# One-hots of the edge stage made on the scalar engine, transposes moved behind the sums

## The chip, the cores and the metric

The kernel runs on one core of a Trainium2 chip. The metric is the device time of one execution in microseconds; 3 runs of the kernel before gave 3189.21, 3190.27 and 3194.09 us. Engine names are those of the profile: PE is the matmul engine (PEld its weight loads), DVE the vector engine, ACT the scalar engine, POOL the GpSimd engine, SP the engine that issues loads.

## What is computed

A layer of a graph network over 6250 nodes of 256 features and 206250 edges. Cut to what matters:

```
edge_index = stack([src, dst]); xn = layernorm(x)
Wh = xn @ W.T + b                                   # 4 heads of 64
e = leaky_relu(alpha_src[i] + alpha_dst[j], 0.2)    # per edge (i, j) and head
att = exp(e - max_i e) / sum_i exp(e - max_i e)
x = x + segment_sum(att * Wh[j], i) + mix(xn)       # mix: linear attention, norms, gelu MLP
x = x + feed_forward(layernorm(x))                  # shared MLP and 2 of 4 experts
```

The mix part and the feed-forward part are dense; the segment sum gathers one row of Wh (and its scores) for each edge.

## The kernel before

A first stage (up to about 630 us of the trace) sorts the edges by blocks of 128 nodes and writes a table of Wh rows. The change is in the second stage, `stage_edges_and_feed_forward`, which works in **lots**: a lot is 8 tiles of 128 edges, all edges of a tile belonging to one node block. There are 234 lots, 6 in an iteration, so 39 iterations. For a lot n:

- POOL (`gathers`, L933) issues 8 indirect DMAs that bring 128 table rows each into one of 6 buffers; it may run 5 lots ahead of the sums.
- `select(n)` makes the lot's one-hot, 128 edges x 8 tiles x 128 nodes, in one of 3 buffers `onehot`: column equal to the edge's node number. Buffer n % 3 comes free when `sums(n - 3)` are done (`s_sum`).
- PE transposes it (`transposes`, L979, 8 matmuls into the bank `turned`), ACT copies it out (`turned_out`, L1182, into `onehot_t`), PE multiplies it by the block's scores (`by_node`, L989), which needs register loads of the block numbers first.
- DVE reduces and adds the scores (`weigh`, L1419 to L1425), ACT takes the exponential (`weights`, L1186), DVE multiplies the gathered rows by it (`product`, L1431, four of them).
- PE loads the bank numbers, clears a bank (`zero`, L995), and adds the lot up with 16 passes of one-hot times rows (`sums`, L1007). ACT copies a bank to `acc` (`block_out`, L1196) when the sums before are done.

Each engine runs its own list in program order. For lot n, `lot` writes into the lists: PE does `by_node(n+1)`, `transposes(n+2)`, a piece, `sums(n)`, a piece; ACT `block_out(n)`, `weights(n)`, `turned_out(n+2)`, two pieces; DVE `weigh(n)`, `select(n+2)`, a piece, `product(n)`, a piece. The pieces are dense work cut into 12 slots, two for each lot of an iteration. A loop over 11 batches (`all_segments`) has in each **round** one iteration with the pieces of a feed-forward batch (slots of `piece`), one with those of a mix batch (`mix`), and the plain iterations, without pieces, that the batch's edges still need: mostly one. Ahead of the loop stand two mix iterations, three plain ones and one feed-forward batch by itself. I call these iterations feed-forward, mix and plain, and number their lots 0 to 5: lot l has the slots 2l and 2l+1.

In the feed-forward iteration slot 4 transposes the normalised batch on PE, ACT copies it out (L1236, L1237), and a long row of matmuls follows. In the mix iteration slot 5 takes a square root on ACT for the first layer norm, which DVE finishes in slot 6 (L1555 to L1562) ahead of the products of lot 3; slot 8 transposes on PE, copies out on ACT and multiplies (L1022), slot 9 goes on with that.

Of the kernel before, what the change touches and what calls it, by code (L numbers as in the profile page):

```python
# [678 lines left out]
def stage_edges_and_feed_forward(nc, A, sh):  # L679
# [4 lines left out]
    with ctx:  # L684
# [16 lines left out]
        ident_bf = sb("ident_bf", [P, P], BF16)  # L701
        zeros = sb("zeros", [1, TB], BF16)
        t24 = sb("t24", [P, NBP, PIECE], BF16)
        t8_rest = dict(half=gathered[:, 0, 0:2, 0:NBP * H].rearrange("p k (b w) -> p b k w", w=H))
# [23 lines left out]
            "w_used", "w_col", "w_rows", "w_kept", "w_in", "w_sel", "w_tr", "w_ot", "w_as", "w_e", "w_exp", "w_sum"))  # L728
        s_dve = sem("s_dve2")

# [238 lines left out]
        def _(pe):  # L969
# [42 lines left out]
            def lot(it, l, piece):  # L1012
                by_node(*after(it, l, 1))
                transposes(*after(it, l, 2))
                piece(2 * l)
                sums(it, l)
                piece(2 * l + 1)

# [155 lines left out]
        def _(act):  # L1174
            s = nc.scalar

            def turned_out(it, l):

                n = number(it, l)
                act.wait_ge(s_tr, n + 1)  # L1180
                wait_freed(act, s_as, n - 1 if not isinstance(n, int) or n else 0)
                s.copy(onehot_t[:, l % 2, :, :].rearrange("p t e -> p (t e)"), turned[:, :]).then_inc(s_ot, 1)  # L1182
# [15 lines left out]
            def lot(it, l, piece):  # L1198
                block_out(it, l)
                weights(it, l)  # L1200
                turned_out(*after(it, l, 2))
                piece(2 * l)
                piece(2 * l + 1)
# [106 lines left out]
            load_mix(TAIL_BATCH)  # L1310
            turned_out(0, 0)
            turned_out(0, 1)
            act.wait_ge(s_w, 16 * LOADS3)
# [4 lines left out]
        def _(dve):  # L1318
# [85 lines left out]
            def select(it, l):  # L1404

                n = number(it, l)
                wait_freed(dve, s_sum, n - 2 if not isinstance(n, int) or n > 2 else 0)
                dve.wait_ge(s_col[l], 16 * it + 16)
                within = col[l][:, :, :, :].rearrange("p g k w -> p (g k) w")[:, :, 1:2].bitcast(F32)
                v.tensor_tensor(onehot[:, l % 3, :, :], iota_row[:, :].unsqueeze(1).broadcast_to([P, TILES, P]),  # L1410
                                within.broadcast_to([P, TILES, P]), ALU.is_equal).then_inc(s_sel[l], 1)

# [256 lines left out]
```

## Time and profile before

| | |
|---|---|
| median of 3 runs | 3190.27 us |
| the profiled execution | 3205.1 us, span 3203.4 us |
| PE busy | 2181.0 us (68%) |
| POOL busy | 2163.3 us (68%) |
| DVE busy | 1919.5 us (60%) |
| ACT busy | 753.7 us (24%) |
| mean granted clock of PE | 0.839 |

The edge stage takes the last 2570 us. Since every engine has a fixed order, busy shares alone do not tell what bounds it: one has to follow a lot from engine to engine in the timeline, and see which wait ends last.

### The profile page before, as it was taken

What the parts mean: (1) busy time and instruction counts of PE and PEld (TensorE: products, weight loads), DVE (VectorE), ACT (ScalarE), POOL (GpSimd) and SP (SyncE); (2) the same over time, 40 slices, a digit from 0 to 9 for tenths busy, and PEclk for the clock granted to TensorE, in tenths of its full rate; (3) what the DMA queues carried; (4) which work ended last, traced back from release to release, by engine and by line L of the source; (5) the groups of instructions that cost most, each with busy time, mean ns of one, the idle gap of its engine ahead of it and who ended that gap; (6) DMA issues with size and microseconds to landing.
All of it is one profiled execution on the core that took longest, in us unless ns stands there. A gap on an engine that the chain in (4) does not pass through costs nothing.

```text
span 3203.4 us, 40657 instructions
## 1 busy us (share of the span) xinstructions
PE 2181.0 (68%) x10817; PEld 1528.2 (48%) x10818; DVE 1919.5 (60%) x3954; ACT 753.7 (24%) x1346; POOL 2163.3 (68%) x2140
## 2 busy tenths in 40 slices
PE   0000687037778868787787978878768787787877
PEld 0000454025555555555555655555555555555554
DVE  8999554036565574656666465575654655756563
ACT  0000343012322222222222222222212222222222
POOL 0003777667777777777777777777777777777770
PEclk6555899568898998888889989898989888899988
DMA  5000122143434444444444434434444344344463
GB/s 183 0 0 1 54 72 66 18 118 91 116 92 105 121 102 123 100 110 113 103 122 101 121 103 104 124 101 123 102 105 123 98 111 117 99 124 102 122 93 31
DMA packets 271533, 305.63 MB, mean 95 GB/s; under 512 B 164258, under 2 KB 210856, under 8 KB 271080
## 3 DMA queue, kind: packets, MB, share of 16 engines
q0 software_dynamic: 97760, 251.60, 30.3%
q1 hardware_dynamic: 140098, 18.08, 3.8%
q10 hardware_dynamic: 33480, 33.36, 3.2%
q8 instruction: 122, 2.00, 0.3%
q14 instruction: 73, 0.60, 0.1%
HBM read 276.25 MB, written 26.62 MB: 95 GB/s over the span
## 4 chain that ended last, share of the span: by engine, by line
PE 34%; POOL 23%; issue 11%; DVE 9%; ACT 1%; DMA 1%; POOLq 0%; DVEq 0%; SPq 0%; ACTq 0%
POOL gathered L933 23%; PE sum_banks L1007 18%; PE f_banks L1022 7%; DVE onehot L1410 3%; PE turned L979 2%; PE f_banks L1066 1%; PE f_banks L1141 1%; DVE gathered L1431 1%; PE sum_banks L995 1%; DMA gathered<-table,col 1%; PE f_banks L1047 1%; PE f_banks L1142 1%; PE f_banks L1048 1%; DVE he L1559 1%; DVE he L1562 1%
## 5 line engine op out<-in xcount | busy, mean ns | idle before, releaser
L933 POOL DMA_INDIRECT gathered<-table,col x1872 | 1904.7, 1017 | 594.7 <-issue 564.5
L1007 PE MATMUL sum_banks<-gathered,onehot 128*128 128x260 f32 x3744 | 1060.8, 445 | 103.2 <-DVE gathered L1431 102.5
L1007 PEld LDWEIGHTS sum_banks<-gathered,onehot 128*128 128x128 f32 x3744 | 818.0, 224 | 292.2 <-issue 129.9
L1431 DVE TENSOR_TENSOR gathered<-gathered 128x512 f32<-128x512 f32 x936 | 591.5, 692 | 46.5 <-ACT gathered L1186 43.7
L1410 DVE TENSOR_TENSOR onehot<-iota_row,col 128x1024 f32<-128x1024 f32 x236 | 288.8, 1224 | 476.0 <-PE sum_banks L1007 447.9
L283 POOL DMA_INDIRECT edge_list<-payload,pos x244 | 247.1, 1013 | 349.9 <-DVE pos L400 273.0
L1182 ACT COPY onehot_t<-turned 128x1024 bf16<-128x1024 bf16 x236 | 238.7, 1011 | 398.0 <-PE turned L979 392.0
L1196 ACT COPY acc<-sum_banks x234 | 88.0, 376 | 870.3 <-PE sum_banks L1007 721.2
L979 PE MATMUL turned<-ident_bf,onehot 128*128 128x128 bf16 x1888 | 158.4, 231 | 188.9 <-DVE onehot L1410 188.8
L979 PEld LDWEIGHTS turned<-ident_bf,onehot 128*128 128x128 bf16 x1888 | 116.1, 103 | 207.0 <-DVE onehot L1410 168.9
L989 PE MATMUL scores<-t,onehot_t 128*128 x1880 | 102.2, 175 | 141.8 <-DVE scored L1419 98.8
L989 PEld LDWEIGHTS scores<-t,onehot_t 128*128 128x128 bf16 x1880 | 86.8, 97 | 219.3 <-issue 200.2
L644 PE MATMUL bank<-ident,y 128*128 128x128 f32 x56 | 8.2, 294 | 234.6 <-DVE y L482 234.6
L1419 DVE TENSOR_REDUCE scored<-scores 128x64 f32<-128x192 f32 x234 | 81.8, 350 | 101.3 <-DMA gathered<-table,col 86.0
L995 PE MATMUL sum_banks<-zeros 1*128 1x260 bf16 x236 | 70.6, 300 | 99.2 <-issue 92.2
L644 PEld LDWEIGHTS bank<-ident,y 128*128 128x128 f32 x56 | 7.0, 153 | 235.3 <-issue 235.3
L1022 PE MATMUL f_banks<-xT,wT_mix 128*128 128x512 f32 x208 | 94.9, 599 | 16.5 <-ACT xT L1294 16.5
L995 PEld LDWEIGHTS sum_banks<-zeros 1*128 1x128 bf16 x236 | 21.7, 92 | 166.2 <-issue 157.7
L1022 PE MATMUL f_banks<-xT,eW 128*128 128x512 f32 (+1 forms) x208 | 90.2, 568 | 0.0
L314 DVE TENSOR_SCALAR_CACHE_REDUCE xn_all<-xn_all,iota_row 128x1612 bf16<-128x1612 bf16 x49 | 88.9, 1891 | 1.8 <-POOL ones_row L273 1.8
L1219 ACT ACTIVATE he<-f_banks,eb 128x512 f32<-128x512 f32 (+1 forms) x78 | 51.3, 661 | 139.1 <-PE f_banks L1022 134.4
L354 DVE TENSOR_TENSOR xn_all<-xn_all 128x1024 f32<-128x1024 f32 x66 | 80.9, 1226 | 2.3
(316 smaller groups left out, 2499.8 us busy)
## 6 DMA issues: line engine op xcount, KB each, us to landing
gathered<-table,col POOLq DMA_INDIRECT x1872
xn_batch<-xn ACTq DMA_DIRECT2D x13, 512.0 KB, 4.4
x_all<-in_x SPq DMA_DIRECT2D x1, 6144.0 KB
x_batch<-in_x ACTq DMA_DIRECT2D x12, 512.0 KB
out<-xf ACTq DMA_DIRECT2D x12, 512.0 KB
edge_list<-xn_all SPq DMA_DIRECT2D x2, 2176.0 KB, 13.7
edge_list<-payload,pos POOLq DMA_INDIRECT x244
col<-edge_list SPq DMA_DIRECT2D x236, 8.0 KB, 2.1
```

Source lines behind the costliest of these rows:

```text
L283: g.indirect_dma_start(sh["windows"], bass.IndirectOffsetOnAxis(ap=pos[:, w:w + 1], axis=0), payload[:, w * Q:w * Q + Q, :].rearrange("p e ...
L314: v.tensor_scalar(hit[b % 2], bucket, iota_row[:, b:b + 1], 0.0, ALU.is_equal, ALU.add, accum_out=counts[:, b:b + 1]).then_inc(s_counts, 1)
L933: g.indirect_dma_start(gathered[:, l, t, :], None, sh["table"], bass.IndirectOffsetOnAxis(ap=col[l][:, t // G, t % G, 0:1], axis=0)).then_ ...
L979: last = t.transpose(turned[:, tile * P:tile * P + P], halves_of[:, l % 3, tile, :, 1], ident_bf[:, :])
L989: last = t.matmul(scores[:, tile * PIECE:tile * PIECE + PIECE], onehot_t[:, l % 2, tile, :], t24[:, ds(blocks[tile // G], 1), :].rearrange ...
L995: return t.matmul(sum_banks[:, bank, 0:TB].rearrange("p a w -> p (a w)"), zeros[:, 0:P], zeros[:, :], start=True, stop=False, skip_group_c ...
L1007: last = t.matmul(sum_banks[:, ds(banks_of[g], 1), 0:TB].rearrange("p a w -> p (a w)"), onehot[:, l % 3, g * G + k, :], gathered[:, l, g * ...
L1022: last = t.matmul(bank, left, right, start=i == 0, stop=i == len(pairs) - 1)
L1182: s.copy(onehot_t[:, l % 2, :, :].rearrange("p t e -> p (t e)"), turned[:, :]).then_inc(s_ot, 1)
L1196: s.copy(acc[:, ds(place, 1), :], sum_banks[:, ds(bank, 1), 0:TB]).then_inc(s_cp, 1)
L1410: v.tensor_tensor(onehot[:, l % 3, :, :], iota_row[:, :].unsqueeze(1).broadcast_to([P, TILES, P]), within.broadcast_to([P, TILES, P]), ALU ...
L1431: v.tensor_tensor(value, value, gathered[:, l, tiles, C:TB].unsqueeze(3).broadcast_to([P, G, H, HD]), ALU.mult).then_inc(s_mul, 1)
```

## The change

The one-hot is no longer made by DVE with one comparison. DVE only writes the negative node numbers of a lot (`minus`, 8 numbers a partition). ACT makes |column - node| tile by tile, 8 activations of 128 columns with a pointer bias into a bf16 buffer `apart`, waits for its own writes, and then takes relu(1 - that) over all 1024 columns into `onehot`. PE transposes lot n+2 behind the sums of lot n, not ahead of them, and ACT's copy of the transposed one-hot stands behind the even piece instead of ahead of it.

```diff
@@ tiles and semaphores
+        apart = sb("apart", [P, TILES, P], BF16)
+        minus = sb("minus", [P, LOTS, TILES, 1])
-        s_dve = sem("s_dve2")
+        s_dve, s_minus, s_apart = sem("s_dve2"), sem("s_minus"), sem("s_apart")
@@ PE
             def lot(it, l, piece):
                 by_node(*after(it, l, 1))
-                transposes(*after(it, l, 2))
                 piece(2 * l)
                 sums(it, l)
+                transposes(*after(it, l, 2))
                 piece(2 * l + 1)
@@ ACT
+            def select(it, l):
+                n = number(it, l)
+                act.wait_ge(s_minus, n + 1)
+                wait_freed(act, s_sum, n - 2 if not isinstance(n, int) or n > 2 else 0)
+                wait_freed(act, s_sel[(l + LOTS - 1) % LOTS], it + 1 if l else it)
+                for tile in range(TILES):
+                    last = s.activation(apart[:, tile, :], iota_row[:, :], ACT.Abs, bias=minus[:, l, tile, :])
+                last.then_inc(s_apart, 1)
+                act.wait_ge(s_apart, n + 1)
+                s.activation(onehot[:, l % 3, :, :], apart[:, :, :], ACT.Relu, bias=1.0, scale=-1.0)\
+                    .then_inc(s_sel[l], 1)
@@ ACT
             def lot(it, l, piece):
                 block_out(it, l)
                 weights(it, l)
+                select(*after(it, l, 2))
+                piece(2 * l)
                 turned_out(*after(it, l, 2))
-                piece(2 * l)
                 piece(2 * l + 1)
@@ ACT, ahead of all lots
-            turned_out(0, 0)
-            turned_out(0, 1)
+            for l in range(2):
+                select(0, l)
+                turned_out(0, l)
@@ DVE
             def select(it, l):
-                wait_freed(dve, s_sum, n - 2 if not isinstance(n, int) or n > 2 else 0)
+                wait_freed(dve, s_sel[l], it)
                 dve.wait_ge(s_col[l], 16 * it + 16)
                 within = col[l][:, :, :, :].rearrange("p g k w -> p (g k) w")[:, :, 1:2].bitcast(F32)
-                v.tensor_tensor(onehot[:, l % 3, :, :], iota_row[:, :].unsqueeze(1).broadcast_to([P, TILES, P]),
-                                within.broadcast_to([P, TILES, P]), ALU.is_equal).then_inc(s_sel[l], 1)
+                v.tensor_scalar(minus[:, l, :, :], within, -1.0, None, ALU.mult).then_inc(s_minus, 1)
```

On PE, before, from the scores of one lot to the sums of the next piece of the list (lot 5 of the mix iteration):

```order
L989 ISA
L989 MATMUL scores<-t,onehot_t 128x24 x2
L979 MATMUL turned<-ident_bf,onehot 128x128 x8
L800 TENSOR_LOAD lots
L995 ISA
L995 MATMUL sum_banks<-zeros 128x260
L1007 ISA
L1007 MATMUL sum_banks<-gathered,onehot 128x260 x2
```

and on PE after, from the scores of the same lot to its first sums:

```order
L991 ISA
L991 MATMUL scores<-t,onehot_t 128x24 x2
L802 TENSOR_LOAD lots
L997 ISA
L997 MATMUL sum_banks<-zeros 128x260
L1009 ISA
L1009 MATMUL sum_banks<-gathered,onehot 128x260 x2
```

The eight transposes have left this place and stand behind the sums, so that the next item of the list, the scores of the following lot, comes straight after them.

On ACT, before, lots 4 and the start of 5 of the mix iteration (L1294 the copies of slot 8, L1298 its gelu):

```order
L1196 COPY acc<-sum_banks 128x260
L1186 ACTIVATE gathered<-e 128x8x4
L1182 COPY onehot_t<-turned 128x1024
L1294 COPY xT<-f_banks 128x512 x2
L1298 ACT_TABLE_LOAD
L1298 ACTIVATE he<-f_banks,b_col 128x512 x2
```

and after:

```order
L1210 COPY acc<-sum_banks 128x260
L1200 ACTIVATE gathered<-e 128x8x4
L1185 ACTIVATE apart<-iota_row,minus 128x128 x8
L1188 ACTIVATE onehot<-apart 128x1024
L1309 COPY xT<-f_banks 128x512 x2
L1313 ACT_TABLE_LOAD
L1313 ACTIVATE he<-f_banks,b_col 128x512 x2
L1196 COPY onehot_t<-turned 128x1024
L802 TENSOR_LOAD lots x2
```

The nine activations of the one-hot stand ahead of the copies that slot 8 waits for, and the copy of the transposed one-hot behind them, right ahead of the next lot's bank copy. The list of ACT holds 39 table loads before and 39 after, at the same neighbours.

## Rows read from the trace of the kernel before

**Rows 1.** Waits: who waited for whom, total us, times, longest us.

```profile
PE turned L979 <- DVE onehot L1410: 188.8, 176, 28.5
...
DVE scored L1419 <- DMA gathered<-table,col: 86.0, 30, 7.8
...
POOL gathered L933 <- PE sum_banks L1007: 30.2, 21, 5.6
...
PE scores L989 <- ACT onehot_t L1182: 3.4, 2, 1.8
```

**Rows 2.** Groups: line, engine, op xcount | busy us, mean ns | idle before, releaser.

```profile
L933 POOL DMA_INDIRECT gathered<-table,col x1872 | 1904.7, 1017 | 594.7 <-issue 564.5 <-PE sum_banks L1007 30.2
```

**Rows 3.** Chain in order of time: start us, us, what.

```profile
1783.63 5.33 PE f_banks L1022 x8
...
1974.77 5.56 PE f_banks L1022 x8
...
2413.61 6.29 PE f_banks L1022 x8
```

**Rows 4.** Timeline of two plain lots: start us, us, engine, line, operation [idle before].

```profile
1539.39 3.77 PE L1007 MATMUL sum_banks<-gathered,onehot 128*128 128x260 f32 x16
...
1543.19 1.23 DVE L1410 TENSOR_TENSOR onehot<-iota_row,col 128x1024 f32<-128x1024 f32 x1 [1.55 <-PE sum_banks L1007]
...
1543.58 0.23 ACT L1186 ACTIVATE gathered<-e 128x32 f32<-128x32 f32 x1
...
1544.48 0.62 PE L979 MATMUL turned<-ident_bf,onehot 128*128 128x128 bf16 x8 [1.13 <-DVE onehot L1410]
1545.13 1.01 ACT L1182 COPY onehot_t<-turned 128x1024 bf16<-128x1024 bf16 x1 [1.32 <-PE turned L979]
...
1545.99 0.28 PE L995 MATMUL sum_banks<-zeros 1*128 1x260 bf16 x1 [0.90 <-issue]
...
1546.21 3.77 PE L1007 MATMUL sum_banks<-gathered,onehot 128*128 128x260 f32 x16
...
1549.82 0.35 PE L989 MATMUL scores<-t,onehot_t 128*128 x8
```

**Rows 5.** Timeline of POOL in the next plain lot.

```profile
1549.35 0.94 POOL L933 DMA_INDIRECT gathered<-table,col  x1 [0.30 <-issue]
1550.60 1.56 POOL L933 DMA_INDIRECT gathered<-table,col  x1 [0.30 <-issue]
```

**Rows 6.** Timeline of the mix iteration, lots 2 and 3.

```profile
1481.10 0.35 PE L989 MATMUL scores<-t,onehot_t 128*128 x8
...
1481.81 1.28 ACT L1186 ACT_TABLE_LOAD   x1
1482.44 0.17 DVE L1555 RECIPROCAL inv<-std 128x4 f32<-128x4 f32 x1
...
1485.40 2.50 DVE L1431 TENSOR_TENSOR gathered<-gathered 128x512 f32<-128x512 f32 x4
...
1486.23 2.14 PE L1007 MATMUL sum_banks<-gathered,onehot 128*128 128x260 f32 x6 [1.84 <-DVE gathered L1431]
```

**Rows 7.** Timeline of the mix iteration, lot 4.

```profile
1491.52 0.35 PE L989 MATMUL scores<-t,onehot_t 128*128 x8
...
1495.95 3.70 PE L1022 MATMUL f_banks<-xT,wT_mix 128*128 128x512 f32 x8 [1.27 <-ACT xT L1294]
```

**Rows 8.** Timeline of the feed-forward iteration, lots 1 and 2.

```profile
1389.59 0.38 ACT L1196 COPY acc<-sum_banks  x1 [4.42 <-PE sum_banks L1007]
...
1394.77 0.59 ACT L1236 COPY xT<-f_banks 128x512 f32<-128x512 f32 x1 [0.69 <-PE f_banks L1059]
```

**Rows 9.** Groups by shape, one on ACT.

```profile
L1219 ACT ACTIVATE he<-f_banks,eb 128x128 f32<-128x128 f32 x6 | 2.0, 367 | 0.3
```

**Rows 10.** Windows, two stretches: us, busy us by engine, granted clock (PEclk).

```profile
1533.00:1556.00 23.00, 18.03 (x116) 14.57 (x117) 15.30 (x33) 4.65 (x10) 17.74 (x18) 1.00 0.42 105
2343.00:2373.00 30.00, 20.67 (x99) 15.34 (x99) 13.67 (x27) 4.48 (x8) 22.99 (x24) 0.83 0.41 104
```

## The prediction

> **What bounds the kernel now.** I read the waits first. POOL, the engine that issues the gathers, waited for PE only 21 times, 30.2 us in all, and DVE waited for a gather before 30 of 234 lots only, 86.0 us [rows 1]. So in most lots the rows are there and the lot waits for the engines. POOL itself needs (1904.7 + 594.7) / 234 = 10.68 us a lot [rows 2], 192 us for the 18 lots of a round of the loop (feed-forward, mix and plain iteration). The chain has the same heavy matmul piece at 1783.63 and 1974.77 [rows 3]: 191.1 us a round. The two are level. What makes POOL quicker brings nothing unless the chain gets quicker too; what lengthens the chain costs in full as soon as the gathers' lead is used.
>
> The chain of a plain lot is in rows 4. Sums start at 1539.39, the next at 1546.21. Behind the sums DVE makes a one-hot (1543.19, 1.23 us), PE waits 1.13 us for it, transposes (0.62), waits 0.90 for its register load, clears the bank and sums. A step is 6.82 us; the register wait is 0.25 us in every other lot, so the mean is 6.5 us. ACT's copy of the transposed one-hot (1545.13, 1.01 us) runs under the sums; the scores waited for it twice in the whole run, 3.4 us [rows 1]. The wait for the one-hot is 188.8 us in all [rows 1]: that is what the change can win.
>
> **The change, part by part.** The diff frees PE from the wait for the one-hot of lot n+2, but puts three things in series that ran under the sums: transposes, ACT's copy, and, through ACT's fixed order, the bank copy and the exponential of the next lot.
>
> *Plain lots.* From the start of the sums: 3.61 us until PE's next item (1546.21 to 1549.82), 0.65 from the start of the transposes to the copy (1544.48 to 1545.13), copy 1.01 [rows 4]: 5.27 us. From there two branches. ACT and DVE: bank copy 0.38 [rows 8], exponential 0.23 [rows 4], first product and its signal 0.83 (1485.40 to 1486.23) [rows 6]: 6.7 us. PE: the scores may start only now, and their register load, till now hidden, is exposed; I price it like the one behind it, 0.25 to 0.90. So 0.25 to 0.90, scores 0.35, 0.25 to 0.90, and 0.22 from clearing to sums [rows 4]: 6.3 to 7.6 us. With the hand-overs between engines I take 7.4, because two loads in series rarely both take the short time: 0.9 us more than 6.5. Bounds 6.7 (the other branch) and 8.0 (long loads, hand-overs of 0.1 to 0.2). Lot 0 behind a branch of the loop waits for instructions anyway and gets nothing: five lots, +4.5 us (1 to 7.5) for a plain iteration.
>
> *The one-hot on ACT.* One activation of 128 columns with a pointer bias took 0.367 us [rows 9], eight 2.9 us, less where they overlap; say 2.2 to 2.9. The relu over 1024 columns is like the copy of 1024, 1.01 us [rows 4]. With the wait between, 3.4 us (3.3 to 4.0). In a plain lot it lies under the sums: ACT is free from 5.9 us to the next copy at 4.3 + 7.4 = 11.7 us, where 3.4 fit. The number of table loads does not change. On DVE 1.23 us goes and a write of 8 numbers comes; DVE bounds nothing there. By the Trainium skill, ScalarE: Activation LUTs, section What ACT_TABLE_LOAD costs, an activation with a pointer bias takes about 280 ns plus 0.833 ns a column and neighbours overlap by 93 ns. As an estimate the one-hot would then be 3.5 us, and the sum the same within 1 us a round; the row of 0.367 us agrees with its 0.387.
>
> *Mix iteration.* Lot 3: from the end of lot 2's sums (1481.10) to lot 3's (1486.23) are 5.13 us [rows 6]. Today ACT has taken the root before that. After, the root stands behind the copy that waits for the transposes: 0.65 + 1.01, table load 1.28, root about 0.2 (like the exponential), then DVE from the reciprocal to the product 2.96 (1482.44 to 1485.40) and 0.83 [rows 4, 6]: 6.95, so +1.8 (1.4 to 2.2). Lot 4: end of sums 1491.52 to the slot's matmuls at 1495.95, 4.43 us [rows 7]. After: 0.65 + 1.01 + 0.38 + 0.23, the one-hot 3.4, two copies of 0.59 that overlap a little (1.1): 6.8, so +2.35 (2 to 3). The transposes behind lot 4's sums add 0.5, since there the matmuls of slot 9 follow at once. Lots 0 to 2 gain about 1.5 us of waits for the one-hot and lose half of it to transposes behind the sums: -0.8. Together +3.8 (2 to 6).
>
> *Feed-forward iteration.* Lot 2: ACT's bank copy at 1389.59 to its copy for slot 4 at 1394.77, 5.2 us [rows 8]. After: 0.65 + 1.01 before the bank copy, then 0.38 + 1.28 + 0.23 + 3.4: 6.95, so +1.7. In lots 3 to 5 two sets of transposes leave a place where PE waited for ACT and stand behind sums with work queued: +0.7. Lots 0 and 1 lose the one-hot's 1.23 us ahead of the products and gain ACT's later start: 0. Together +2.3 (1 to 4).
>
> *Sum.* A round gets 4.5 + 3.8 + 2.3 = 10.6 us longer; 11 rounds +117. Ahead of the loop stand two mix and three plain iterations: 2 x 3.8 + 3 x 4.5 = 21, of which 4 fall where lots wait for gathers today: +17. One round has one more plain iteration: 2413.61 - 1974.77 = 438.8 us for two rounds [rows 3] leaves 56.6 for it, 9.4 a lot, the pace of the gathers. A late chain finds its rows waiting and takes 6 x 7.4 = 44: -12. The last lot waits 7.8 us for its gathers today [rows 1], not then: -7. In all +115. The span of 3203.4 becomes 3318; the profiled execution stands 14.8 us over the median, so the forecast is 3190 + 115 = **3305 us**. With the low bounds a round costs 4 and the total is +25 (3215); with the high ones 17.5 and +208 (3398).
>
> **Rivals.** *Faster.* POOL's gathers are stretched where DVE works from two SBUF tiles: 0.94 us each, but 1.56 for one beside a one-hot (1550.60) [rows 5]. All stretches together are 1904.7 - 1872 x 0.94 = 145 us [rows 2], and I give the one-hots two thirds, 90 us. If the chain shortens by its 188.8 us of waits and gains none, POOL is the bound and the time 3190 - 90 = 3100. It decides at a plain lot of 6.5 us: the mechanism wins only if scores and register loads behind ACT's copy take less than the 1.13 us that PE waits now. Against it: the copy alone is 1.01 and nothing covers it. Chance 0.11. The Trainium skill, SBUF — State Buffer, section Who interferes with whom, holds that two SBUF inputs on DVE contend with GpSimd's reads but infers that descriptor generation goes on. By that, this rival's gain from POOL would be nil and its time about 3190; the trace's 1.56 us speaks against it.
>
> *No change* (0.04): low bounds everywhere, and a faster pace of the gathers in the first rounds: 3190.
>
> *A colder PE* (0.15). In plain lots that follow each other closely the granted clock is 1.00 with PE busy 18.03 of 23 us; in plain lots that wait for gathers it is 0.83, busy 20.67 of 30 [rows 10]. PE's share in my 7.4 us lot is (3.61 + 0.62 + 0.35 + 0.28) / 7.4 = 66%, nearer to the second. There a lot costs PE 20.67 / 3 = 6.9 us instead of 18.03 x 6.5 / 23 = 5.1: 1.8 more in about 70 plain lots, 3305 + 126 = 3430.
>
> **How the numbers follow.** The forecast's case, the chain longer at full clock, has 0.70. The range of 3215 to 3440 takes in its bounds and the colder case; it leaves out faster, no change (together 0.15) and 0.05 above. A measurement tells 0.2%, 6 us, from no change. Faster 0.11, same 0.04, slower 0.85.
>
> **What would show it.** Right: scores waiting for ACT's copy more than 200 us in all, against 3.4; POOL waiting for the sums in every round; the wait of transposes for the one-hot near zero; plain steps of about 7.4 us; a round of about 202 us; gathers mostly 0.94 us without being worth anything. Wrong: if plain steps stay at 6.5 (faster), if the one-hot takes over 5 us and the transposes wait for it (slower than the range), or if ACT's register loads and not its activations fill its period.

## The result and the profile after

The changed kernel takes **3595.52 us** (median of 4 runs, 3590.64 to 3601.07), the kernel before 3191.26 beside it (3189.21 to 3194.09): a ratio of 1.1267, 95% interval 1.1247 to 1.1287. The direction was forecast, the size was not: +404 us instead of +115, and outside the range.

The profiled execution has a span of 3596.0 us. Below: busy time by engine, then the groups, of the changed kernel (operation, xcount | busy us, mean ns | idle before, releaser). In the changed file the gathers are L935, transposes L981, scores L991, zeroing L997, sums L1009, one-hots L1185 and L1188, ACT's copy of the turned one-hots L1196, the exponential L1200, the bank copy L1210.

```profile
PE 2368.9 (66%) x10817; PEld 1664.8 (46%) x10818; DVE 1667.7 (46%) x3954; ACT 1551.5 (43%) x3470; POOL 2093.5 (58%) x2140
```

```profile
L935 POOL DMA_INDIRECT gathered<-table,col x1872 | 1835.0, 980 | 1039.7 <-issue 535.5 <-PE sum_banks L1009 504.1
...
L1009 PE MATMUL sum_banks<-gathered,onehot 128*128 128x260 f32 x3744 | 1172.1, 481 | 154.0 <-DVE gathered L1446 152.2
...
L1185 ACT ACTIVATE apart<-iota_row,minus 128x128 bf16<-128x128 f32 x1888 | 574.3, 389 | 36.1 <-DVE minus L1426 36.0
```

And the same group of the sums before the change:

```profile
L1007 PE MATMUL sum_banks<-gathered,onehot 128*128 128x260 f32 x3744 | 1060.8, 445 | 103.2 <-DVE gathered L1431 102.5
```

The gathers became a little shorter (980 ns against 1017, [rows 2]) and worth nothing, for POOL now waits for the sums: 504.1 us against 30.2 [rows 1]. The same 3744 matmuls of the sums cost 111 us more; their number and shape are unchanged, and the windows below show the clock. The waits after (who for whom: total us, times, longest):

```profile
PE scores L991 <- ACT onehot_t L1196: 220.3, 128, 2.1
...
PE sum_banks L997 <- issue: 121.5, 114, 1.4
...
DVE recip L1478 <- ACT acc L1210: 87.8, 11, 8.4
...
PE turned L981 <- ACT onehot L1188: 33.3, 2, 31.0
```

and the row of the zeroing before the change:

```profile
PE sum_banks L995 <- issue: 92.2, 137, 1.0
```

The wait of the transposes for one-hots is down from 188.8 us to 33.3 (nearly all of it once, at the start), the wait of the scores for ACT's copy is up from 3.4 to 220.3 [rows 1], and DVE has a new wait for ACT, 8 us in each round. PE's wait for its own queue ("issue") ahead of the zeroing is not new; it rose by 29 us in all, so where it matters has to be read lot by lot. The chain of the kernel after, which answers to [rows 3]:

```profile
1748.74 6.10 PE f_banks L1024 x8
...
2417.74 6.11 PE f_banks L1024 x8
...
2700.42 6.42 PE f_banks L1024 x8
```

From the first to the second row are three rounds, (2417.74 - 1748.74) / 3 = 223.0 us each, against 191.1. Two plain lots of the kernel after, PE and one ACT row, which answer to [rows 4] (start us, us, engine, line, operation, [idle before]):

```profile
1670.54 0.28 PE L997 MATMUL sum_banks<-zeros 1*128 1x260 bf16 x1 [1.34 <-issue]
1670.76 5.46 PE L1009 MATMUL sum_banks<-gathered,onehot 128*128 128x260 f32 x16
...
1676.05 0.61 PE L981 MATMUL turned<-ident_bf,onehot 128*128 128x128 bf16 x8
1676.70 1.01 ACT L1196 COPY onehot_t<-turned 128x1024 bf16<-128x1024 bf16 x1 [4.80 <-PE turned L981]
...
1678.34 0.58 PE L991 MATMUL scores<-t,onehot_t 128*128 x8 [1.68 <-ACT onehot_t L1196]
...
1679.59 0.28 PE L997 MATMUL sum_banks<-zeros 1*128 1x260 bf16 x1 [0.67 <-issue]
1679.90 3.77 PE L1009 MATMUL sum_banks<-gathered,onehot 128*128 128x260 f32 x16
```

The order is the predicted one: sums, transposes, copy, scores, zeroing, in series. Two sizes are not. The zeroing waits 1.34 or 0.67 us behind the scores for nothing but PE's own queue ("issue"), and the first of these two sums takes 5.46 us instead of 3.77. Windows inside it (us; busy PE, PEld, DVE, ACT, POOL; granted clock, DMA share, GB/s):

```profile
1670.70:1671.70 1.00, 1.00 (x5) 0.86 (x5) 0.93 (x4) 0.97 (x2) 0.69 (x2) 1.00 0.41 133
...
1672.70:1673.70 1.00, 1.00 (x4) 0.81 (x3) 0.00 (x0) 0.00 (x0) 0.88 (x1) 0.50 0.44 83
...
1675.70:1676.70 1.00, 0.96 (x11) 0.63 (x9) 0.00 (x0) 0.00 (x1) 0.69 (x2) 1.00 0.44 133
```

The clock is at its upper level, 2.4 GHz, when the sums begin, falls to 1.2 GHz about a microsecond later, and is back before the sums end. In the 3.80 us ahead of these sums PE was busy for 0.77 us only, and the granted clock there was still 1.00.

What PE waits for under "issue" is a register load. These are PE's and ACT's loads in the kernel before (duration min/median/max in ns):

```profile
L800 ACTq TENSOR_LOAD <-lots x468: 271/278/1437, 689.3 to 3140.5; - x156
...
L800 PEldq TENSOR_LOAD <-blk x235: 327/332/348, 687.2 to 3149.9; - x118
L800 PEldq TENSOR_LOAD <-lots x234: 585/1030/1255, 691.6 to 3151.8; - x117
```

PE's load of the bank numbers (`lots`) took 0.585 to 1.255 us before the change too. There the transposes of 0.62 us lay over it. The Trainium skill, DMA: Bandwidth & Descriptors, section Latency and other measured facts, gives a tensor_load a floor of about 600 ns; the shortest loads of `lots` agree, those of `blk` at 327 ns and ACT's at 271 ns lie below it, so here it is no floor.

The two durations of the `lots` load follow the number of the lot. In both kernels all 117 loads of odd-numbered lots take 1.23 to 1.26 us, and those of even-numbered lots 0.58 to 0.61 us (a few, all in lot 0 of an iteration, up to 1.10). In the plain iterations of the changed kernel the lots with the long load, 1, 3 and 5, have sums of 5.46 us, and lots 2 and 4, with the short one, nearly always 3.77; lot 0, behind the loop's branch, has 5.46 too.

Where the 404 us stand. Counted from one lot's last sums matmul to the next one's in the timeline, medians of rounds 3 to 7 of the 11 (us a lot, six lots an iteration; the last column is the mean of the iterations):

| iteration | before | after | sum before, after |
|---|---|---|---|
| feed-forward | 11.3 8.5 18.2 11.5 8.9 15.0 | 14.3 9.8 23.8 11.6 9.4 14.7 | 73.3, 84.1 |
| mix | 9.7 14.9 11.5 10.4 11.9 17.4 | 12.3 13.3 13.1 13.5 15.6 16.5 | 75.7, 84.3 |
| plain | 8.7 6.8 6.2 6.9 6.4 6.8 | 9.7 9.7 7.5 9.8 7.4 10.2 | 42.1, 54.2 |

The two profiled executions differ by 392.6 us. Lots 0 to 29, ahead of the loop, end at 1041.5 us instead of 986.6: +55. Nearly all the rest, some 335 us, is in the loop, 30.5 a round.

### The profile page after: what moved, and what is told of

It is laid out like the page before. It is cut to its first block, busy times and chain, and to the rows that moved or that the text cites. A ratio compares the mean times of both kernels' runs of the same rounds, so it can differ in the third digit from the quotient of the medians.

```text
span 3596.0 us, 43078 instructions
## 1 busy us (share of the span) xinstructions
PE 2368.9 (66%) x10817; PEld 1664.8 (46%) x10818; DVE 1667.7 (46%) x3954; ACT 1551.5 (43%) x3470; POOL 2093.5 (58%) x2140
## 4 chain that ended last, share of the span: by engine, by line
PE 56%; issue 9%; ACT 7%; DVE 6%; ACTq 3%; POOL 1%; DVEq 0%; DMA 0%; SPq 0%; POOLq 0%
PE sum_banks L1009 32%; PE f_banks L1024 9%; PE turned L981 3%; ACT onehot_t L1196 3%; PE f_banks L1068 2%; PE scores L991 2%; ACTq L802 2%; ACT apart L1185 2%; DVE gathered L1446 2%; PE f_banks L1143 1%; PE sum_banks L997 1%; POOL gathered L935 1%; PE f_banks L1049 1%; PE f_banks L1144 1%; PE f_banks L1047 1%
## 5 line engine op out<-in xcount | busy, mean ns | idle before, releaser
L935 POOL DMA_INDIRECT gathered<-table,col x1872 | 1835.0, 980 | 1039.7 <-issue 535.5
L1009 PE MATMUL sum_banks<-gathered,onehot 128*128 128x260 f32 x3744 | 1172.1, 481 | 154.0 <-DVE gathered L1446 152.2
L1009 PEld LDWEIGHTS sum_banks<-gathered,onehot 128*128 128x128 f32 x3744 | 893.1, 244 | 379.7 <-issue 182.2
L1196 ACT COPY onehot_t<-turned 128x1024 bf16<-128x1024 bf16 x236 | 238.9, 1012 | 1006.7 <-PE turned L981 1006.7
L1185 ACT ACTIVATE apart<-iota_row,minus 128x128 bf16<-128x128 f32 x1888 | 574.3, 389 | 36.1 <-DVE minus L1426 36.0
L991 PE MATMUL scores<-t,onehot_t 128*128 x1880 | 132.7, 178 | 330.8 <-ACT onehot_t L1196 220.3
L991 PEld LDWEIGHTS scores<-t,onehot_t 128*128 128x128 bf16 x1880 | 99.7, 98 | 407.9 <-issue 399.0
L1188 ACT ACTIVATE onehot<-apart 128x1024 f32<-128x1024 bf16 x236 | 249.4, 1057 | 7.5
L997 PE MATMUL sum_banks<-zeros 1*128 1x260 bf16 x236 | 69.1, 294 | 172.1 <-issue 121.5
L981 PE MATMUL turned<-ident_bf,onehot 128*128 128x128 bf16 x1888 | 144.8, 220 | 33.3 <-ACT onehot L1188 33.3
L981 PEld LDWEIGHTS turned<-ident_bf,onehot 128*128 128x128 bf16 x1888 | 125.7, 98 | 69.1 <-ACT onehot L1188 33.9
L1210 ACT COPY acc<-sum_banks x234 | 87.8, 375 | 112.3 <-issue 112.0
L1024 PE MATMUL f_banks<-xT,wT_mix 128*128 128x512 f32 x208 | 115.5, 706 | 26.2 <-ACT xT L1309 26.2
L997 PEld LDWEIGHTS sum_banks<-zeros 1*128 1x128 bf16 x236 | 21.6, 92 | 226.1 <-issue 218.5
L1610 DVE TENSOR_TENSOR he<-f_banks,he 128x512 f32<-128x512 f32 x26 | 16.7, 686 | 221.2 <-PE f_banks L1144 221.2
L1024 PE MATMUL f_banks<-xT,eW 128*128 128x512 f32 (+1 forms) x208 | 93.0, 584 | 0.0
```

What stands on the lines that cost most here:

```text
L935: g.indirect_dma_start(gathered[:, l, t, :], None, sh["table"], bass.IndirectOffsetOnAxis(ap=col[l][:, t // G, t % G, 0:1], axis=0)).then_ ...
L981: last = t.transpose(turned[:, tile * P:tile * P + P], halves_of[:, l % 3, tile, :, 1], ident_bf[:, :])
L991: last = t.matmul(scores[:, tile * PIECE:tile * PIECE + PIECE], onehot_t[:, l % 2, tile, :], t24[:, ds(blocks[tile // G], 1), :].rearrange ...
L997: return t.matmul(sum_banks[:, bank, 0:TB].rearrange("p a w -> p (a w)"), zeros[:, 0:P], zeros[:, :], start=True, stop=False, skip_group_c ...
L1009: last = t.matmul(sum_banks[:, ds(banks_of[g], 1), 0:TB].rearrange("p a w -> p (a w)"), onehot[:, l % 3, g * G + k, :], gathered[:, l, g * ...
L1024: last = t.matmul(bank, left, right, start=i == 0, stop=i == len(pairs) - 1)
```

## The experiments

Every run is timed beside the kernel before. The first four have two measured times each, the others four or ten.

### Order and engine apart

**The order alone**: the kernel before, with two moves and DVE's one-hots.

```
 PE:   by_node(*after(it, l, 1))
-      transposes(*after(it, l, 2))
       piece(2 * l)
       sums(it, l)
+      transposes(*after(it, l, 2))
       piece(2 * l + 1)
 ACT:  weights(it, l)
-      turned_out(*after(it, l, 2))
       piece(2 * l)
+      turned_out(*after(it, l, 2))
```

> The kernel before with the change's order alone: transposes behind the sums on PE, the copy of the transposed one-hot behind the even piece on ACT; the one-hots stay on DVE. Theory A (the order puts copy, bank copy and exponential in series behind every lot's sums, and the gaps bring PE to its low clock): plain steps of 7.4 and 9.8 us in turn as in the changed kernel, only the two places where ACT's one-hot delays a piece (2.3 and 1.7 us a round) fall away: 3500 to 3560 us. Theory B (ACT's new load of 3.4 us a lot is what costs, the order is free): 3190 to 3260 us.

Measured: 3564.51 us, ratio 1.1147 (1.1103 to 1.1191). The order alone costs some 370 us of the 404, with DVE making the one-hots. Plain iterations take 58.0 us, more than with ACT's one-hots (54.2); more of their sums run at the lower clock (1215.5 us of sums in all, against 1172.1).

**The one-hots alone**: the changed kernel with PE's and ACT's old order (transposes ahead of the sums, copy ahead of the even piece).

> The one-hots on ACT alone, with the order of the kernel before: PE transposes lot n+2 ahead of the sums of lot n and so waits for ACT's nine activations. Theory A: a plain step is sums 3.6, bank copy 0.4, exponential 0.2, one-hot 3.4, transposes 0.65, register load and clearing 0.5 to 1.1: 9 to 9.5 us in every plain lot, 3600 to 3750 us; moving the transposes was then the lesser evil. Theory B (order is free either way, the load alone costs): the time of the changed kernel, 3595 us within 1%.

Measured: 4144.72 us, ratio 1.2961 (1.2921 to 1.3002), far above both ranges: A had the direction and not the size. A line of its waits:

```profile
PE turned L981 <- ACT onehot L1188: 905.7, 223, 31.4
```

ACT's one-hots stand behind ACT's exponential of the lot, and the transposes, then the sums, wait for them: the order of the change is needed for its engine. Alone, each half costs more than nothing; the two losses don't add.

**A lighter one-hot**: one absolute value instead of eight, its result used for all eight tiles, so that the edges of seven of eight tiles go to wrong nodes.

```
-  for tile in range(TILES):
-      last = s.activation(apart[:, tile, :], iota_row[:, :], ACT.Abs, bias=minus[:, l, tile, :])
+  last = s.activation(apart[:, 0, :], iota_row[:, :], ACT.Abs, bias=minus[:, l, 0, :])
```

> The changed kernel with one absolute value of 128 columns instead of eight, read eight times by the relu: all tiles of a lot get the one-hot of tile 0, so the sums go to wrong nodes, the work of every other instruction is the same. ACT does 2.1 us less a lot. Theory A: plain steps stay; two places a round get about 2 us back: 3595 - 50 = 3545 us. Theory B: at least half of the loss comes back: under 3400 us.

Measured: 3611.7 us (3604.92 to 3618.48), in neither range and 16 us above the changed kernel. Two microseconds a lot less on ACT bring nothing in all, but two things go against each other in it. Lot 2 of the feed-forward falls from 23.8 to 21.3 us. Plain iterations rise from 54.2 to 57.0 us, with the sums of lots 2 and 4 at the lower clock too (1236.2 us of sums in all, against 1172.1). ACT's activations don't seem to fill the plain lots, but this run didn't hold the clock still, and why it was lower isn't shown.

### The clock

**Extra matmuls behind the transposes**, 10 of 240 columns into an unused bank, in plain lots.

> The changed kernel with ten matmuls of 240 bf16 columns into an unused bank behind the transposes of each plain lot, in the gap where PE waits for ACT's copy (about 1 us of work at full clock, 2 us at half). If the long plain steps of 9.8 us are those of 7.4 at PE's low clock, brought on by the gaps: all steps about 7.4 to 7.6 us, 15 plain iterations x 8 us less: 3460 to 3500 us. If they are long for another reason (register loads): 3595 us or more.

Measured: 3586.32 us, and plain lots as before, 9.7 and 7.4 us. A miss. The matmuls ran at full clock right behind the transposes, while ACT copied; the wait behind the scores stayed empty, and the fall came all the same, in the same lots, a microsecond into the sums. So I filled both.

```
+  def filler(slot):
+      for i in range(8 if slot % 2 else 6):
+          t.matmul(f3[:, 0:10 * PIECE], ident_bf[:, :],
+                   t24[:, 0:10, :].rearrange("p a w -> p (a w)"), start=True, stop=True)
```

> The changed kernel with extra matmuls into an unused bank in the lots of the plain iterations: 8 of 240 columns behind the transposes and 6 behind the scores of each lot (the run before had 10 behind the transposes alone, where the clock fell all the same, some 1 us after the sums had begun). Nothing waits for them. Theory A (the clock falls for the idle gap behind the scores): the sums of the plain lots take 3.77 us in all lots and not 5.46 in four of six, minus about 0.4 us a lot for matmuls that the gap doesn't cover; about 1.2 us a lot less over some 75 plain lots and the 12 of the added iterations: 3480 to 3530 us. Theory B (the share of time with matmuls doesn't set the clock here): 3590 to 3640 us.

Measured: 3559.2 us, ratio 1.1153 (1.1125 to 1.118), 36 us under the changed kernel; plain iterations 50.9 us instead of 54.2. PE in plain lots of this run, then a window over them:

```profile
1667.57 0.78 PE L1175 MATMUL f_banks<-t,ident_bf 128*128 128x240 bf16 x6
...
1668.63 3.77 PE L1009 MATMUL sum_banks<-gathered,onehot 128*128 128x260 f32 x16
...
1676.42 0.28 PE L997 MATMUL sum_banks<-zeros 1*128 1x260 bf16 x1 [0.69 <-issue]
1676.73 3.77 PE L1009 MATMUL sum_banks<-gathered,onehot 128*128 128x260 f32 x16
```

```profile
1661.00:1690.00 29.00, 24.75 (x174) 19.80 (x174) 11.99 (x33) 17.31 (x41) 22.30 (x23) 1.00 0.42 105
```

With both gaps filled the clock holds, and the sums take 3.77 us. Such a lot takes 7.4 us with the short load and 8.1 with the long one (1668.63 to 1676.73). This is the plain lot without its clock loss. The 9.7 us and 9.8 us of lots 1 and 3 of the changed kernel are these 8.1 plus 5.46 - 3.77 = 1.7. Lots 0 and 5 stay at 9.7 and 10.2 us, with sums of 5.46 us as in the changed kernel. The gain is 36 us and not the 65 to 115 that A expected.

### The register loads

**Both loads at the top of the lot**, ahead of the wait for the turned one-hots.

```
 PE:
+      banks, blocks = banks_for(it, l), blocks_of(*after(it, l, 1))
-      by_node(*after(it, l, 1))
+      by_node(*after(it, l, 1), blocks)
       piece(2 * l)
-      sums(it, l)
+      sums(it, l, banks)
```

> The changed kernel with one thing moved: TensorE's two register loads of a lot (the block numbers for the scores of lot n+1, the bank numbers for the sums of lot n) are issued at the top of the lot, ahead of the wait for the turned one-hots, and not each right ahead of its use. In the trace of the changed kernel the load of the bank numbers stands open between scores and zeroing (0.59 us or 1.24 us a lot, 0.94 mean, 234 times), the load of the block numbers (0.33 us, with its overhead 0.62) between ACT's copy and the scores. Before the change the eight transposes lay over the first of them. Theory A (what I had not priced is these loads on the chain): 1.0 to 1.6 us less a lot, so 3220 to 3360 us, and the steps of the plain lots fall from 9.7/7.4 to 7.9/6.2 or so. Theory B (the chain only shows the loads, the sums wait for products and the clock does the rest): 3540 to 3600 us.

Measured: 3442.81 us, ratio 1.0788 (1.0766 to 1.0809): 153 us less, two thirds of the least that A expected. Plain iterations fall from 54.2 to 44.6 us. PE there:

```profile
1606.96 3.77 PE L1014 MATMUL sum_banks<-gathered,onehot 128*128 128x260 f32 x16 [0.42 <-DVE gathered L1452]
1610.57 0.61 PE L981 MATMUL turned<-ident_bf,onehot 128*128 128x128 bf16 x8
1612.37 0.59 PE L998 MATMUL scores<-t,onehot_t 128*128 x8 [1.19 <-ACT onehot_t L1202]
1612.89 0.28 PE L1004 MATMUL sum_banks<-zeros 1*128 1x260 bf16 x1
1613.59 3.77 PE L1014 MATMUL sum_banks<-gathered,onehot 128*128 128x260 f32 x16 [0.42 <-DVE gathered L1452]
```

Nothing stands between scores and zeroing any more, the clock holds though no matmul was added, and the next wait is for DVE's products: a step of 6.63 us, which is the other branch of the prediction (copy, bank copy, exponential, first product: 6.7). I had expected more because I had left this branch out of the expectation.

**The same in the kernel before** (its own order, loads at the top).

> The kernel before the change, with TensorE's two register loads at the top of each lot as in the run with early words. The waits of TensorE in the kernel before have 92.2 us (137 times) in which the zeroing waits for nothing but this load, and 39.5 us ahead of the scores. Theory A (TensorE's chain bounds the lots of the kernel before too): 60 to 100 us less, 3090 to 3135 us. Theory B (GpSimd's gathers bound it where the loads stand, as I held in the prediction): 3175 to 3195 us. Then the loads cost only where the changed order makes TensorE the last.

Measured: 3209.71 us, ratio 1.0057 (1.0041 to 1.0074): 18 us more than the kernel before, and 15 above B's range. Plain iterations fall from 42.1 to 38.9 us, feed-forward iterations rise from 73.3 to 77.8. A line of the waits:

```profile
DVE scored L1425 <- DMA gathered<-table,col: 181.6, 56, 8.7
```

In the kernel before that wait was 86.0 us in 30 lots [rows 1]. What PE gained in plain lots, the kernel spends waiting for rows: nearer to theory B, in that a quicker chain wins nothing from the kernel before. Why it costs 18 us, and why the feed-forward iteration grows, isn't shown. Moving the loads pays in the changed order alone.

### The chain scores, copy, transposes

**Scores behind the sums**: PE does sums of n, scores of n+1, transposes of n+2, and ACT copies the turned one-hots of n+1 ahead of making those of n+2. Then no lot waits for its own transposes.

```
 PE:   piece(2 * l)
       sums(it, l)
+      by_node(*after(it, l, 1))
       transposes(*after(it, l, 2))
 ACT:  weights(it, l)
+      turned_out(*after(it, l, 1))
       select(*after(it, l, 2))
       piece(2 * l)
-      turned_out(*after(it, l, 2))
```

> The changed kernel in another order: on TensorE sums of lot n, scores of lot n+1, transposes of lot n+2; on ACT the copy of the turned one-hots of lot n+1 ahead of the one-hots of lot n+2. So the scores don't wait for a copy that waits for transposes behind the sums; the chain of a lot is sums 3.77, block numbers 0.35, scores 0.6, four DVE operations 1.0, exp 0.23, first product 0.7: about 6.6 us instead of 7.4 to 9.8. Theory A (the chain through transposes, copy and register loads is the loss, the one-hots on ACT are not): 3130 to 3300 us. Theory B (one-hots on ACT cost by themselves, ACT 43% busy against 24%): 3400 us or more.

Measured: 3377.94 us, ratio 1.0584 (1.0565 to 1.0604), 218 us less than the changed kernel, but 80 more than A's upper end. Plain iterations now take 40.6 us, less than before the change (42.1); feed-forward and mix still take 84.8 and 83.0.

**The same with DVE's one-hots.**

> The order of the run before (scores behind the sums, transposes behind the scores, copy of the turned one-hots a lot later) with the one-hots made by DVE as before the change. It tells what the one-hots on ACT are worth where the order doesn't hide it. DVE's one-hots (2.4 us a lot by rows 3 and 4) then stand between the scores and the products of the lot or beside them: if they lie on the chain, 0.5 to 1 us a lot more than with ACT's, so 100 to 230 us above the run before; if they don't, within 30 us of it.

Measured: 3388.71 us, ratio 1.0601 (1.057 to 1.0632): equal to ACT's within 11 us, but made up otherwise. (The 2.4 us a lot in the expectation is a mistake: a one-hot of DVE takes 1.23 us by [rows 4].) Plain iterations take 52.2 us, since DVE's one-hot stands between scores and products; feed-forward 81.3, lot 2 of it 18.2 as before the change against 24.3. ACT's one-hots gain in plain lots and lose in the others.

**Scores behind the sums and early loads together.**

> The changed one-hots (ACT) with the order scores behind sums, and the register loads at the top of the lot. The order alone gave 3377.94 us with plain lots of 6.2 to 7.9 us. Theory A (the loads cover each other's place): the register loads are behind transposes there already, so 10 to 40 us less, 3335 to 3370 us. Theory B (what is left, some 180 us above the kernel before, comes from the loads): below 3250 us.

Measured: 3371.57 us, ratio 1.0562 (1.0544 to 1.0579): 6 us less than the order alone, which the runs can't tell from nothing, and less than A's 10 to 40. Where the scores don't wait and the transposes lie over the load, moving the loads wins next to nothing. The two repairs mend the same place.

### The pieces behind ACT's one-hots

**The even piece ahead of the one-hots on ACT**, everything else as in the changed kernel.

> The changed kernel with one thing moved on ACT: the even piece of the feed-forward or mix ahead of the one-hots of the lot, and not behind them. The prediction gave the one-hots ahead of the transposed input 1.7 us in lot 2 of the feed-forward; the traces show 23.8 us for that lot against 20.6 with the same order and DVE's one-hots. Theory A (the rest of the loss over the order alone is ACT's one-hots ahead of pieces): that lot falls to about 20.6 us, and the whole to 3545 to 3575 us (the order alone took 3564.51). Theory B (the one-hots then delay the transposes by as much): 3585 to 3605 us.

Measured: 3573.0 us, ratio 1.1201 (1.1182 to 1.122): 23 us less, as A. Lot 2 of the feed-forward falls from 23.8 to 20.6 us, which is its length with the order alone. The place in the changed kernel:

```profile
1516.39 2.43 ACT L1185 ACTIVATE apart<-iota_row,minus 128x128 bf16<-128x128 f32 x8
...
1518.85 1.06 ACT L1188 ACTIVATE onehot<-apart 128x1024 f32<-128x1024 bf16 x1
...
1520.28 0.59 ACT L1252 COPY xT<-f_banks 128x512 f32<-128x512 f32 x1
...
1520.92 1.01 PE L1068 MATMUL f_banks<-gW,xT 128*128 128x4 f32 x4 [4.11 <-ACT xT L1252]
```

PE waits 4.1 us for copies that stand behind 3.5 us of one-hots. **All three moves together**:

> ACT's one-hots, scores behind sums, register loads at the top of the lot, and the even piece ahead of the one-hots on ACT. Theory A (the three losses add up: lot 2 of the feed-forward 24.3 to 20 us or so, 11 times, and lots 4 and 5 of the mix 1 to 2 us each): 60 to 90 us below the run without the last step, about 3270 to 3310 us. Theory B (a lot of the feed-forward or mix then ends with another wait): less than 20 us below it.

Measured: 3285.36 us, ratio 1.0292 (1.0275 to 1.031), 86 us below the run without the last step: A. Mix iterations are back at 76.1 us, feed-forward not: 81.7. Its chain in a feed-forward iteration (start us, us, what):

```profile
1424.59 2.44 ACT apart L1191 x8
...
1427.05 1.07 ACT onehot L1194
...
1428.16 0.62 PE turned L981 x8
1428.78 6.94 PE f_banks L1030 x16
```

Dense matmuls, ACT's piece, one-hots, transposes, dense matmuls: PE's odd piece is queued behind transposes that nobody needs so early. **The transposes behind the odd piece**:

```
       by_node(*after(it, l, 1), blocks)
-      transposes(*after(it, l, 2))
       piece(2 * l + 1)
+      transposes(*after(it, l, 2))
```

> The run with all three repairs and one move more on TensorE: the transposes of lot n+2 behind the odd piece of lot n, and not ahead of it. In its trace the chain of a feed-forward round runs ACT piece, one-hots on ACT (2.44 + 1.07 us), transposes (0.62), TensorE's odd piece, up to four times. Theory A (that chain is the remaining loss): the feed-forward iteration falls from 81.7 to 71 to 75 us and the kernel to 3190 to 3230 us, where the gathers bound it. Theory B (the rest lies elsewhere, in the boundary of the iterations or the clock): 3265 to 3300 us.

Measured: **3187.96 us**, ratio 0.9978 (0.9968 to 0.9988; 10 runs beside 19 of the kernel before). The iterations take 75.5, 73.9 and 42.1 us. That is A, with the iteration 0.5 us above its range and the kernel 2 us below; the last 94 us are gone. Its chain, then POOL's group:

```profile
1972.85 5.40 PE f_banks L1030 x8
...
2163.87 5.46 PE f_banks L1030 x8
```

```profile
L935 POOL DMA_INDIRECT gathered<-table,col x1872 | 1842.0, 984 | 635.8 <-issue 555.9 <-PE sum_banks L1014 79.9
```

A round is 191.0 us, as before the change. The kernel is 408 us quicker than the changed one, and quicker than the kernel before by 0.2%, which is at the edge of what the runs can tell.

**The one-hots behind both pieces on ACT**:

> As the run before, and ACT's one-hots behind both pieces of the lot instead of between them. If ACT's odd pieces waited behind the one-hots, 10 to 30 us less than the run before; if ACT's odd pieces wait for late work of TensorE and hold up the one-hots, 20 to 100 us more. I take the second for a little likelier, since in the feed-forward ACT's odd piece waits for a product of the same lot of TensorE.

Measured: 3465.44 us, ratio 1.0836 (1.0813 to 1.0858), 277 us more: the sign I leaned to, at three times its upper end. PE then waits 255.2 us, 61 times, for the one-hots, since ACT's odd pieces wait for others: its activations of the experts' layers (`he`, L1240) wait 269.7 us for dense matmuls, against 188.1 in the run before, and 129.3 us of waits for DVE's `xf` now stand ahead of the one-hots.

**The same order with DVE's one-hots**, behind the products:

> The order of the run with the transposes last, with DVE's one-hots (as before the change) put behind the products of the lot. Theory A (the one-hots on ACT have a value once the order hides them: DVE's one-hots stretch gathers, 1.56 against 0.94 us, and TensorE's order is equal): 20 to 60 us above the run with ACT's. Theory B (the engine is indifferent, gathers bound both): within 15 us of it.

Measured: 3191.55 us, ratio 0.9978 (0.9967 to 0.999): theory B: in this order the engine that makes the one-hots makes no difference. POOL's group here:

```profile
L933 POOL DMA_INDIRECT gathered<-table,col x1872 | 1891.4, 1010 | 594.3 <-issue 556.5 <-PE sum_banks L1012 37.8
```

DVE's one-hots stretch the gathers by 1891.4 - 1842.0 = 49 us in all. With ACT's, POOL waits 79.9 - 37.8 = 42 us longer for PE instead. That leaves 7, and the medians differ by 4, with intervals that overlap.

## Why the prediction was right or wrong

**Right: what bounds, and the mechanism.** "The two are level" held both ways: a quicker chain in the kernel before (early loads) won nothing, gathers that took 49 us less (ACT's one-hots in the last order, against DVE's) won 4, and the order that lost nothing on PE returned to 191 us a round. The three things put in series are the ones in the trace. Four signs named beforehand came: scores waiting over 200 us (220.3), POOL waiting in every round, transposes hardly waiting, gathers mostly 0.94 us. Two did not: plain steps are near 7.4 us in two lots of six only, and a round is 223.0 us, not 202. The faster rival was rightly small. Its 90 us for shorter gathers were too many: the group fell by 1904.7 - 1835.0 = 70 us, and by 49 between two kernels of one order.

**Where it failed.** By the chain a round is 31.9 us longer and not 10.6. The table has it as plain +12.1 (+4.5 forecast), mix +8.6 (+3.8) and feed-forward +10.8 (+2.3). Three terms of the sum were too small, for three reasons: the register loads of the plain lots, the lower clock, which the forecast put at nothing, and the feed-forward's baseline.

**Wrong: the register load, as the prediction priced it** ("I price it like the one behind it, 0.25 to 0.90"). That range is what stood open in [rows 4] behind 0.62 us of transposes, and the change takes those away: an uncovered remainder was used as the price of an operation. The load's own duration, 0.585 to 1.255 us, was in the trace of before, the long one in every odd-numbered lot. Open, it costs 0.67 or 1.34 us, and the load of the block numbers about 0.6. At full clock the plain steps are therefore 7.4 and 8.1 (the filled run), with 7.4 the lower value and not the middle. Issuing the loads early gave 153 us, the clock that came with it included.

**Wrong: the colder PE as a rival of 0.15.** It came, and beside the longer chain, not in its place: PE was busy 187.9 us more with the same 10817 instructions (2368.9 us, 2181.0 before). The price of such a lot was near, 1.8 us estimated and 1.7 measured. But the clock isn't the whole miss: with it the prediction had 3430, 166 below the measured time, and filling the gaps of the plain lots won 36 us. The prediction itself found its lot nearer to the row with clock 0.83 than to that with 1.00, and still left the forecast at full clock. The longer gap of the exposed load and the lower clock are not independent: with the loads early the clock held without any filler. It also looked for the lower clock in the wrong places: in the plain iterations lots 1, 3 and 5 fell, some 40 lots that stood at the upper clock before, and not 70, but the mix and feed-forward iterations lost too. The sums lost 111 us in the whole kernel, and the same matmuls of the mix (L1024 in lot 4, 3.70 us in [rows 7]) took 5.21.

**The mix iteration**: +3.8 predicted, +8.6 measured. The chain of lot 3 came out at 1611.03 to 1618.00, 6.97 us for 6.95; lot 4's copies at 6.59 for 6.8. The rows after:

```profile
1611.03 0.61 PE L981 MATMUL turned<-ident_bf,onehot 128*128 128x128 bf16 x8
...
1618.00 6.71 PE L1009 MATMUL sum_banks<-gathered,onehot 128*128 128x260 f32 x16 [2.25 <-DVE gathered L1446]
...
1624.54 0.61 PE L981 MATMUL turned<-ident_bf,onehot 128*128 128x128 bf16 x8
...
1631.13 5.21 PE L1024 MATMUL f_banks<-xT,wT_mix 128*128 128x512 f32 x8 [1.94 <-ACT xT L1309]
```

What was missed are the durations at the lower clock in both, and lots 0 to 2: -0.8 predicted, +2.6 measured (+2.6, -1.6 and +1.6). That these lots have the chain of the plain lots too is the likely reason; they weren't traced one by one.

**The feed-forward iteration**: +2.3 predicted, +10.8 measured. Lot 2: +1.7 predicted, +5.6 measured. The step that failed is its baseline. [rows 8] are from the first round of the loop, where PE got to its small matmuls (L1066) only at 1395.89, 6.5 us behind the sums of lot 1; the lot took 20.5 us. In the later rounds it is otherwise. Before and after, in a later round, where the sums of lot 1 end at 1966.06 and 2182.11:

```profile
1970.08 0.61 PE L1066 MATMUL f_banks<-gW,xT 128*128 128x4 f32 x4 [1.20 <-ACT xT L1237]
```

```profile
2189.97 1.01 PE L1068 MATMUL f_banks<-gW,xT 128*128 128x4 f32 x4 [4.12 <-ACT xT L1252]
```

4.0 us have become 7.9, +3.8, where I had 5.2 and 6.95 for ACT. The length of ACT's chain was right in its terms; what it replaces was read from a round that isn't typical. The rest, 1.8 us, are small matmuls of 1.01 us in place of partly 0.61 and the dense ones behind them (6.1 us for 5.6), the clock again. The run with the pieces first took 3.2 us off this lot. Lot 0: 0 predicted, +2.9 measured. That lot 0 "behind a branch of the loop waits for instructions anyway", as the prediction has it for the plain iteration, overlooked ACT's branch:

```profile
1489.61 1.01 ACT L1196 COPY onehot_t<-turned 128x1024 bf16<-128x1024 bf16 x1 [4.87 <-PE turned L981]
...
1494.64 0.38 ACT L1210 COPY acc<-sum_banks  x1 [4.03 <-issue]
...
1495.29 0.17 DVE L1478 TENSOR_SCALAR recip<-acc 128x16 f32 x1 [7.70 <-ACT acc L1210]
```

ACT takes its 4 us of branch and loads only behind the copy, which now waits for transposes behind the sums, and DVE's normalisation waits for ACT. Before the change DVE had no such wait. With the copy moved earlier (scores behind the sums) it fell from 87.8 to 24.4 us.

**Ahead of the loop**: +17 predicted, +55 measured, by the same steps of 9.7 us. **The extra plain iteration**: by the chain, one round with it is 2700.42 - 2417.74 = 282.7 us, less 223.0 leaves 59.7 us, where 44 were forecast and 56.6 stood before; the credit of 12 us did not exist, because its lots take 7.4 to 10.6 us, 9.6 in the mean, and not 7.4.

**The one-hot on ACT** was priced right: eight in 2.43 us for 2.2 to 2.9, with the relu 3.5 us.

**What stays open.** Why the load of `lots` takes 0.59 us in even lots and 1.24 in odd ones isn't shown. A row of that table has 6 words, so that every second row starts 8 bytes past a multiple of 16, counted from the table's start. PE reads 5 words of it, of `blk` 4 words, always at a multiple of 16, and ACT one word at a time. No run changes the row's length. How the 153 us divide between the load and the clock that came with it is only an estimate: plain iterations take 50.9 us with the gaps filled and 44.6 with the loads early, so of the 9.6 us won there some 3.3 would be clock and 6.3 load. Whether the early loads are needed beside the other moves wasn't tried without them. The mended kernel still has sums at the lower clock (1074.3 us in all against 1060.8), and its time doesn't show it.

## What to carry to other kernels

When a change takes the cover off an operation, price it by its own duration in the trace (register loads and branches too, which no busy time shows), never by the wait that was left while it was covered. When new waits open between the matmuls of a dense engine, add up the sum once with the durations of full clock and once with those of the lower clock, and don't leave the second to a rival of small chance: a gap can cost once as a gap and again in the matmuls behind it. And where two engines are level, a reordering must leave every other queue alone: here the time came back only with four moves (scores, loads, the one-hots behind ACT's piece, the transposes behind PE's odd piece), of which the loads may not be needed, and then the change was worth next to nothing.

## What was not expected of the hardware

- The clock fell about 1 us after the sums had begun, in a stretch with PE fully busy (1.00, then 0.50), so the price of a gap is paid by the work behind it: 5.46 us for 3.77. Filling the first of two gaps left the same lots at 5.46 us, filling both held the clock at 1.00 over 29 us.
- PE's register load of 4 words took 0.33 us from one table. Its load of 5 words from another took 0.59 us in even-numbered lots and 1.24 us in odd-numbered ones, without exception for the odd. ACT's loads of one word from that second table took 0.278 us in the median.
- Eight activations of 128 columns with a bias by pointer, one behind the other, took 2.43 us together, 389 ns each.
